# Graph attention heads on one core: one exponential instruction per unit instead of two halves

## The chip, the cores and the metric

The kernel runs on one core of a Trainium2 chip. The metric is the device time in microseconds (us) of one execution; the lower the better.

## The reference, cut to what matters

A graph of 3125 nodes and 103125 edges passes through a graph attention layer with 8 heads, a routed mixture of experts, three more attention layers and a gated feed-forward layer. The change touches only the first attention layer:

```
e = e_left[src] + e_right[dst]
e = jnp.where(e >= 0, e, NEG_SLOPE * e)
e_max = segment_max(e, dst, num_segments=N)
e_exp = jnp.exp(e - e_max[dst])
denom = segment_sum(e_exp, dst, num_segments=N)
alpha = e_exp / (denom[dst] + EPS)
out = segment_sum(Wh[src] * alpha[:, :, None], dst, num_segments=N)
```

## The kernel before, in words

The kernel treats the graph as a dense matrix: a row for each destination node, a column for each source node (3136 columns, NS), and a mask that holds the logarithm of the number of edges between the two. The stage `heads_phase` computes the softmax over the columns and multiplies it with the projected nodes `hx`.

The work is cut into 50 blocks: two passes of 4 heads each (HG), and in each pass 25 blocks of 128 destination nodes. Each head of a block is a unit, so there are 200 units. A unit goes through these steps:

- VectorE, `maxima(u)`: one instruction forms the scores of all 3136 columns into one of three buffers `sc` (L944), and one adds the mask and takes the row's extreme (L948). It first waits until TensorE has transposed the unit that had this buffer three units ago (`s_T`).
- ScalarE, `exps(u, j)`: the exponentials in place, in two halves (L904). Half 0 holds 1664 columns (13 tiles of 128), half 1 holds 1472. Each instruction also leaves the sum of its row in `den`.
- TensorE, `transposes(n)` (L996): the 25 tiles of a unit are turned in four groups of 7, 6, 6 and 6 (TG), n = 4u + gi, into two PSUM buffers `psT` by turns.
- ScalarE, `copy_out(u, gi)` (L913): copies a group from `psT` to `probsT`, two buffers as well.
- TensorE, `products(n)` (L1010): multiplies the copied group into `psO`.

Every engine works through its own queue in a fixed order. TensorE takes `transposes(n + 1)` and then `products(n)`. `transposes(n)` waits until the copy of group n - 2 is out of its buffer; `products(n)` waits for the copy of group n. ScalarE takes, in unit u, copy 0, copy 1, half 0 of the exponentials of unit u + 1, copy 2, copy 3, half 1 of unit u + 1:

```
for gi in range(4):
    copy_out(u, gi)
    if gi % 2 == 1 and u + 1 < UNITS:
        exps(u + 1, gi // 2)
```

VectorE runs two units ahead. Once in a block, after the maxima, `sums(B)` adds the two halves of the denominators (L955), takes their reciprocal (L957) and copies the block's sums out of PSUM into `sumsT` (L959). TensorE turns these with 8 small multiplications (`transpose_sums`, L1017), which stand in its queue behind the last products of the first unit of the next block. `rows(B)` (L967) multiplies with the reciprocals, and GpSimd stores the block.

Of the kernel before, what the change touches and what calls it, by code (L numbers as in the profile page):

```python
# [8 lines left out]
ALU = mybir.AluOpType  # L9
ACT = mybir.ActivationFunctionType  # L10
AX = mybir.AxisListType

P = 128
# [8 lines left out]
NS = SA * SC  # L22
# [14 lines left out]
HG = P // CH  # L37
# [780 lines left out]
CUT = T0[2] * P  # L818
# [4 lines left out]
def heads_phase(nc, g, hx, el, mask, y_dram):  # L823

    with ExitStack() as ctx:
        sb = lambda n, s, d=F32: ctx.enter_context(nc.sbuf_tensor(f"hd_{n}", s, d))
        sem = lambda n: new_semaphore(nc, g, f"hd_{n}")
        sc = sb("scores", [P, 3, NS])
        lv = sb("loops", [LOOP_R[1], 4, LOOP_Q])
        pT = sb("probsT", [P, 2, 7 * P])  # L830
        nm = sb("negmax", [P, 3])
        den = sb("den", [P, 3, HG, 2])
        rden = sb("rden", [P, 3, HG])
        spare = sb("spare", [1, 1])
        oT = sb("sumsT", [P, HG, P])
# [2 lines left out]
        psT = [ctx.enter_context(nc.psum_tensor(f"hd_psT{i}", [P, 1024], F32)) for i in range(2)]  # L838
        psO = [ctx.enter_context(nc.psum_tensor(f"hd_psO{i}", [P, 512], F32)) for i in range(3)]
        psY = ctx.enter_context(nc.psum_tensor("hd_psY", [P, 512], F32))  # L840
        names = ("s_leaky", "s_nm", "s_exp", "s_turned", "s_copied", "s_products", "s_sum", "s_rden", "s_y", "s_oT", "s_yT",
                 "s_fold", "s_loop_in", "s_loop_exp", "s_loop_plus_one", "s_loop_ln", "s_loop_new", "s_loop_out", "s_loop_kept")
        s_lk, s_nm, s_ex, s_T, s_ev, s_mm, s_sum, s_rd, s_y, s_oT, s_yT, s_fold, s_lin, s_lexp, s_lone, s_lln, s_lneg, s_lout, s_lkept = (
            sem(n) for n in names)
        s_mask = [sem(f"s_mask{i}") for i in range(2)]
        s_store = [sem(f"s_store{i}") for i in range(3)]
# [3 lines left out]
        UNITS = BLOCKS * HG  # L850
        CG = P // CH
        LOOP_UNIT = 6
        assert LOOP_UNIT + 1 < HG * (L1_LOOPS // P - 2)
        halves = (slice(0, CUT), slice(CUT, NS))

        def load_el(eng, q, h, i):

# [37 lines left out]

        @block.scalar
        def _(act):
            def exps(u, j):
                B, k = u // HG, u % HG
                if j == 0:  # L900
                    act.wait_ge(s_nm, u + 1)
                    if k == 0 and B >= 3:
                        act.wait_ge(s_y, B - 2)
                nc.scalar.activation(sc[:, u % 3, halves[j]], sc[:, u % 3, halves[j]], ACT.Exp, scale=-1.0,  # L904
                                     bias=nm[:, u % 3:u % 3 + 1], accum_out=den[:, B % 3, k, j:j + 1]).then_inc(s_ex, 1)

            def copy_out(u, gi):
                n = u * 4 + gi
                act.wait_ge(s_T, n + 1)
                if n >= 2:  # L910
                    act.wait_ge(s_mm, n - 1)
                w = TG[gi] * P
                nc.scalar.activation(pT[:, gi % 2, 0:w], psT[gi % 2][:, 0:w], ACT.Copy).then_inc(s_ev, 1)  # L913

            exps(0, 0)
            exps(0, 1)
            for u in range(UNITS):
                if u == LOOP_UNIT:
                    act.wait_ge(s_lin, 16)
                    nc.scalar.activation(lv[:, 1, :], lv[:, 0, :], ACT.Exp, scale=-1.0).then_inc(s_lexp, 1)  # L920
                if u == LOOP_UNIT + 1:
                    act.wait_ge(s_lone, 1)
                    nc.scalar.activation(lv[:, 2, :], lv[:, 2, :], ACT.Ln).then_inc(s_lln, 1)
                for gi in range(4):
                    copy_out(u, gi)
                    if gi % 2 == 1 and u + 1 < UNITS:
                        exps(u + 1, gi // 2)

        @block.vector
        def _(dve):  # L930
            nc.vector.tensor_reduce(fold[:, :], g["ident"][:, :].rearrange("p (j c) -> p c j", c=CH), AX.X,
                                    ALU.add).then_inc(s_fold, 1)

            def maxima(u):
                B, h, c = u // HG, u % HG, u % 3
                q, b = B // NB, B % NB
                if h == 0 and B >= 2:
                    dve.wait_ge(s_mask[B % 2], 16 * (B // 2))
                if b == 0 and q:
                    dve.wait_ge(s_el[h], 32 * q)  # L940
                if u >= 3:
                    dve.wait_ge(s_T, 4 * (u - 2))
                o = D + q * HG + h
                nc.vector.scalar_tensor_tensor(sc[:, c, :], el[:, h, 0, :], hx[:, b, o:o + 1], el[:, h, 1, :],  # L944
                                               ALU.subtract, ALU.min).then_inc(s_lk, 1)
                dve.wait_ge(s_lk, u + 1)
                nc.vector.memset(spare[:, :], 0.0)
                nc.vector.tensor_tensor_reduce(out=sc[:, c, :], in0=sc[:, c, :], in1=mask[:, B % 2, :],  # L948
                                               scale=1.0, scalar=3.0e38, op0=ALU.add, op1=ALU.min,
                                               accum_out=nm[:, c:c + 1]).then_inc(s_nm, 1)  # L950

            def sums(B):
                i = B % 3
                dve.wait_ge(s_ex, (B + 1) * HG * 2)
                nc.vector.tensor_tensor(rden[:, i, :], den[:, i, :, 0], den[:, i, :, 1], ALU.add).then_inc(s_sum, 1)  # L955
                dve.wait_ge(s_sum, B + 1)
                nc.vector.reciprocal(rden[:, i, :], rden[:, i, :]).then_inc(s_rd, 1)  # L957
                dve.wait_ge(s_mm, (B + 1) * HG * 4)
                nc.vector.tensor_copy(oT[:, :, :].rearrange("p h n -> p (h n)"), psO[i][:, 0:HG * P]).then_inc(s_oT, 1)  # L959

            def rows(B):
                i = B % 3
                dve.wait_ge(s_yT, B + 1)
                dve.wait_ge(s_rd, B + 1)
                if B >= 3:
                    dve.wait_ge(s_store[i], 16 * (B // 3))
                nc.vector.tensor_tensor(y[:, i, :].rearrange("p (h c) -> p h c", h=HG),  # L967
                                        psY[:, 0:P].rearrange("p (h c) -> p h c", h=HG),
                                        rden[:, i, :].rearrange("p (h o) -> p h o", o=1).broadcast_to([P, HG, CH]),
                                        ALU.mult).then_inc(s_y, 1)  # L970
            maxima(0)
            maxima(1)
            for u in range(UNITS):
                if u + 2 < UNITS:
                    maxima(u + 2)
                if u % HG == 0 and u:
                    sums(u // HG - 1)
                elif u % HG == 1 and u > HG:
                    rows(u // HG - 1)
            sums(BLOCKS - 1)  # L980
            rows(BLOCKS - 1)

        @block.tensor
        def _(pe):
            pe.wait_ge(s_fold, 1)

            def transposes(n):
                u, gi = n // 4, n % 4
                if gi % 2 == 0:
                    pe.wait_ge(s_ex, u * 2 + gi // 2 + 1)  # L990
                if n >= 2:
                    pe.wait_ge(s_ev, n - 1)
                for t in range(TG[gi]):
                    c0 = (T0[gi] + t) * P
                    r = min(P, NS - c0)
                    last = nc.tensor.transpose(psT[gi % 2][0:r, t * P:(t + 1) * P], sc[:, u % 3, c0:c0 + r], g["ident"][:, :])  # L996
                last.then_inc(s_T, 1)

            def products(n):
                u, gi = n // 4, n % 4  # L1000
                B, h = u // HG, u % HG
                pe.wait_ge(s_ev, n + 1)
                if gi == 0 and h == 0 and B >= 3:
                    pe.wait_ge(s_y, B - 2)
                c0 = (B // NB * HG + h) * CH
                for t in range(TG[gi]):
                    tt = T0[gi] + t
                    r = min(P, NS - tt * P)
                    cg = tt % CG
                    last = nc.tensor.matmul(psO[B % 3][cg * CH:(cg + 1) * CH, h * P:(h + 1) * P], hx[0:r, tt, c0:c0 + CH],  # L1010
                                            pT[0:r, gi % 2, t * P:(t + 1) * P], start=tt < CG, stop=tt >= sum(TG) - CG)
                last.then_inc(s_mm, 1)

            def transpose_sums(B):
                pe.wait_ge(s_oT, B + 1)
                for h in range(HG):
                    last = nc.tensor.matmul(psY[:, h * CH:(h + 1) * CH], oT[:, h, :], fold[:, :], start=True, stop=True)  # L1017
                last.then_inc(s_yT, 1)
            transposes(0)
            for n in range(UNITS * 4):  # L1020
                if n + 1 < UNITS * 4:
                    transposes(n + 1)
                products(n)
                if n % (4 * HG) == 3 and n > 4 * HG:
                    transpose_sums(n // (4 * HG) - 1)
            transpose_sums(BLOCKS - 1)
# [1111 lines left out]
```

## Time and profile before

| | |
|---|---|
| median of 3 runs | 3909.28 us (3903.76 to 3923.56) |
| profiled execution, its own time | 3912.36 us |
| its span | 3910.7 us |
| busy: PE, DVE, ACT, POOL | 3470.7, 2890.0, 2387.8, 233.7 us |
| granted TensorE clock, mean over the span | 0.959 |
| heads stage, first score instruction to last | 520.0 to 1945.5 us |

PE is TensorE, PEld its loading of weights, DVE VectorE, ACT ScalarE, POOL GpSimd. The engines run beside each other, so busy times don't add up to the span. A clock of 1.00 is the 2.4 GHz level, 0.50 the 1.2 GHz level; other values are means over a stretch.

### The profile page before, as it was taken

How to read it: one execution, taken by the hardware profiler on the slowest of the kernel's cores; microseconds unless marked ns; L12 is line 12 of the kernel's file. 1: busy time of each engine (PE TensorE's matmuls, PEld its weight loads, DVE VectorE, ACT ScalarE, POOL GpSimd, SP SyncE). 2: the span in 40 equal slices, each digit the busy share in tenths (PEclk: the TensorE clock that was granted, in tenths of full speed). 3: DMA queues.
4: the chain of work that ended last, by engine and by line, in shares of the span. 5: the costliest groups of instructions: out<-in, count | busy, mean ns of one | idle time of the engine just before them, and what ended most of it. 6: DMA issues, size and time to landing. Idle time of an engine off the chain costs nothing. (4 is left out here: it accounts for less than half of the span.)

```text
span 3910.7 us, 69756 instructions
## 1 busy us (share of the span) xinstructions
PE 3470.7 (89%) x27387; PEld 2703.4 (69%) x27388; DVE 2890.0 (74%) x4413; ACT 2387.8 (61%) x3738; POOL 233.7 (6%) x230
## 2 busy tenths in 40 slices
PE   4998978888888889888937999699999999999699
PEld 3555546666666666666636899688878887888577
DVE  5999999999999999999853222465556555555485
ACT  3777778888888888888810011266656665444432
POOL 1000000000000000000002444100000000000010
PEclk8999999999999999999958999899999999999899
DMA  3423211111115111111166787332323322333210
GB/s 98 184 99 126 100 65 54 70 53 56 67 53 202 53 70 53 55 68 53 37 215 204 217 240 199 91 130 106 109 71 128 114 101 78 137 116 116 66 56 33
DMA packets 153038, 404.77 MB, mean 104 GB/s; under 512 B 20453, under 2 KB 98664, under 8 KB 134664
## 3 DMA queue, kind: packets, MB, share of 16 engines
q1 hardware_dynamic: 133682, 360.65, 26.4%
q0 software_dynamic: 15552, 36.16, 3.9%
q8 instruction: 223, 3.65, 0.4%
q10 hardware_dynamic: 3478, 3.46, 0.3%
q14 instruction: 103, 0.84, 0.1%
HBM read 335.03 MB, written 65.19 MB: 102 GB/s over the span
## 5 line engine op out<-in xcount | busy, mean ns | idle before, releaser
L913 ACT ACTIVATE hd_probsT<-hd_psT 128x768 f32<-128x768 f32 (+1 forms) x800 | 649.1, 836 | 183.8 <-PE hd_psT L996 183.0
L996 PE MATMUL hd_psT<-ident,hd_scores 128*128 128x128 f32 (+1 forms) x5000 | 737.9, 286 | 12.8 <-ACT hd_scores L904 12.8
L944 DVE SCALAR_TENSOR_TENSOR hd_scores<-el_heads,hx 128x3136 f32<-128x3136 f32 x200 | 695.6, 3478 | 0.0
L948 DVE CUSTOM_DVE_ANT_0 hd_scores<-hd_scores,mask_heads 128x3136 f32<-128x3136 f32 x200 | 684.1, 3420 | 8.6
L1010 PE MATMUL hd_psO<-hd_probsT,hx 128*32 128x128 f32 (+1 forms) x10000 | 582.9, 286 | 98.3 <-ACT hd_probsT L913 97.6
L996 PEld LDWEIGHTS hd_psT<-ident,hd_scores 128*128 128x128 f32 (+1 forms) x5000 | 544.3, 143 | 166.7 <-issue 164.5
L904 ACT ACTIVATE hd_scores<-hd_scores,hd_negmax 128x1664 f32<-128x1664 f32 (+1 forms) x400 | 640.7, 1602 | 8.2 <-DVE hd_negmax L948 8.1
L1458 PE MATMUL ly_psO<-hx_a,ly_probsT 128*128 128x256 f32 x2500 | 583.7, 381 | 0.0
L1416 ACT ACTIVATE ly_probsT<-ly_psT 128x768 f32<-128x768 f32 (+1 forms) x300 | 249.6, 832 | 469.0 <-PE ly_psT L1447 468.8
L1010 PEld LDWEIGHTS hd_psO<-hd_probsT,hx 128*32 128x32 f32 (+1 forms) x10000 | 322.6, 110 | 296.9 <-ACT hd_probsT L913 173.6
L1458 PEld LDWEIGHTS ly_psO<-hx_a,ly_probsT 128*128 128x128 f32 x2500 | 453.8, 189 | 71.3 <-issue 16.6
L480 DVE TENSOR_SCALAR onehot_c<-iotaC,stage_c 128x392 bf16<-128x392 f16 x1200 | 295.0, 315 | 0.0
L1458 PE MATMUL ly_psO<-hx_b,ly_probsT 128*128 128x256 f32 x1250 | 292.0, 381 | 0.0
L538 PE MATMUL cnt<-onehot_c,onehot_dst_a 128*128 128x392 bf16 x1200 | 236.8, 334 | 52.4 <-DVE onehot_c L480 52.4
L1447 PE MATMUL ly_psT<-ident,ly_scores 128*128 128x128 f32 x1875 | 258.3, 276 | 16.7 <-ACT ly_scores L1407 16.7
L538 PEld LDWEIGHTS cnt<-onehot_c,onehot_dst_a 128*128 128x128 bf16 x1200 | 135.2, 128 | 171.4 <-issue 76.2
L1407 ACT ACTIVATE ly_scores<-ly_scores,ly_negmax 128x1664 f32<-128x1664 f32 (+1 forms) x150 | 239.6, 1597 | 20.5 <-DVE ly_negmax L1303 10.4
L1303 DVE CUSTOM_DVE_ANT_0 ly_scores<-ly_scores,ly_mask 128x3136 f32<-128x3136 f32 x73 | 249.7, 3420 | 3.1
L1458 PEld LDWEIGHTS ly_psO<-hx_b,ly_probsT 128*128 128x128 f32 x1250 | 226.8, 189 | 35.6 <-issue 8.3
L1447 PEld LDWEIGHTS ly_psT<-ident,ly_scores 128*128 128x128 f32 x1875 | 219.0, 141 | 44.1 <-ACT ly_scores L1407 17.2
L1817 PEld LDWEIGHTS moe_ps_h<-moe_xT,moe_w 128*128 128x128 f32 x2048 | 241.3, 194 | 5.5 <-DVE moe_xT L1858 2.3
L1852 ACT ACTIVATE moe_hidden<-moe_ps_h 128x512 f32<-128x512 f32 x64 | 38.2, 597 | 337.0 <-PE moe_ps_h L1817 263.2
(328 smaller groups left out, 3902.6 us busy)
## 6 DMA issues: line engine op xcount, KB each, us to landing
ly_mask<-mask_dram SPq DMA_DIRECT2D x75, 1568.0 KB, 6.6
mask_heads<-mask_dram SPq DMA_DIRECT2D x48, 1568.0 KB, 7.0
moe_w<-in_L_ffn_w SPq DMA_DIRECT2D x144, 512.0 KB
mask_dram<-logc SPq DMA_DIRECT2D x200, 196.0 KB, 1.9
el_heads<-el_dram POOLq DMA_DIRECT2D x4, 1568.0 KB, 19.1
el_heads<-el_slope_dram POOLq DMA_DIRECT2D x4, 1568.0 KB, 22.7
el_heads<-el_dram SPq DMA_DIRECT2D x4, 1568.0 KB, 11.5
el_heads<-el_slope_dram SPq DMA_DIRECT2D x4, 1568.0 KB, 14.9
```

The source lines that it names most:

```text
L480: last = nc.vector.tensor_scalar(oc[:, k, :], g["iotaC"][:, :], c[:, k:k + 1], None, ALU.is_equal)
L538: last = nc.tensor.matmul(o, ohA[:, s, :, k], ohC[:, s, k, :], start=k == 0 and not further, stop=True, skip_group_check=True)
L904: nc.scalar.activation(sc[:, u % 3, halves[j]], sc[:, u % 3, halves[j]], ACT.Exp, scale=-1.0, bias=nm[:, u % 3:u % 3 + 1], accum_out=den[: ...
L913: nc.scalar.activation(pT[:, gi % 2, 0:w], psT[gi % 2][:, 0:w], ACT.Copy).then_inc(s_ev, 1)
L944: nc.vector.scalar_tensor_tensor(sc[:, c, :], el[:, h, 0, :], hx[:, b, o:o + 1], el[:, h, 1, :], ALU.subtract, ALU.min).then_inc(s_lk, 1)
L948: nc.vector.tensor_tensor_reduce(out=sc[:, c, :], in0=sc[:, c, :], in1=mask[:, B % 2, :], scale=1.0, scalar=3.0e38, op0=ALU.add, op1=ALU.m ...
L996: last = nc.tensor.transpose(psT[gi % 2][0:r, t * P:(t + 1) * P], sc[:, u % 3, c0:c0 + r], g["ident"][:, :])
L1010: last = nc.tensor.matmul(psO[B % 3][cg * CH:(cg + 1) * CH, h * P:(h + 1) * P], hx[0:r, tt, c0:c0 + CH], pT[0:r, gi % 2, t * P:(t + 1) * P ...
L1303: nc.vector.tensor_tensor_reduce(out=sc[:, c, :], in0=sc[:, c, :], in1=mask[:, B % 2, :], scale=1.0, scalar=3.0e38, op0=ALU.add, op1=ALU.m ...
L1416: nc.scalar.activation(pT[:, gi % 2, 0:w], psT[gi % 2][:, 0:w], ACT.Copy).then_inc(s_ev, 1)
L1447: last = nc.tensor.transpose(psT[gi % 2][0:r, t * P:(t + 1) * P], sc[:, B % 3, c0:c0 + r], g["ident"][:, :])
L1458: last = nc.tensor.matmul(psO[B % 2][:, 0:D], pT[0:r, gi % 2, t * P:(t + 1) * P], hx[B // NB % 2][0:r, tt, 0:D], start=tt == 0, stop=tt == ...
```

## The change

The exponentials of a unit become one instruction over all 3136 columns, issued where half 0 stood, behind the second copy. The denominators have one value for each head, so the addition in `sums` and its semaphore go. TensorE waits once per unit for the exponentials, ahead of its first group of transposes.

```diff
-        den = sb("den", [P, 3, HG, 2])
+        den = sb("den", [P, 3, HG])
...
-            def exps(u, j):
+            def exps(u):
                 B, k = u // HG, u % HG
-                if j == 0:
-                    act.wait_ge(s_nm, u + 1)
-                    if k == 0 and B >= 3:
-                        act.wait_ge(s_y, B - 2)
-                nc.scalar.activation(sc[:, u % 3, halves[j]], sc[:, u % 3, halves[j]], ACT.Exp, scale=-1.0,
-                                     bias=nm[:, u % 3:u % 3 + 1], accum_out=den[:, B % 3, k, j:j + 1]).then_inc(s_ex, 1)
+                act.wait_ge(s_nm, u + 1)
+                if k == 0 and B >= 3:
+                    act.wait_ge(s_y, B - 2)
+                nc.scalar.activation(sc[:, u % 3, :], sc[:, u % 3, :], ACT.Exp, scale=-1.0,
+                                     bias=nm[:, u % 3:u % 3 + 1], accum_out=den[:, B % 3, k:k + 1]).then_inc(s_ex, 1)
...
-            exps(0, 0)
-            exps(0, 1)
+            exps(0)
...
-                    if gi % 2 == 1 and u + 1 < UNITS:
-                        exps(u + 1, gi // 2)
+                    if gi == 1 and u + 1 < UNITS:
+                        exps(u + 1)
...
-                dve.wait_ge(s_ex, (B + 1) * HG * 2)
-                nc.vector.tensor_tensor(rden[:, i, :], den[:, i, :, 0], den[:, i, :, 1], ALU.add).then_inc(s_sum, 1)
-                dve.wait_ge(s_sum, B + 1)
-                nc.vector.reciprocal(rden[:, i, :], rden[:, i, :]).then_inc(s_rd, 1)
+                dve.wait_ge(s_ex, (B + 1) * HG)
+                nc.vector.reciprocal(rden[:, i, :], den[:, i, :]).then_inc(s_rd, 1)
...
-                if gi % 2 == 0:
-                    pe.wait_ge(s_ex, u * 2 + gi // 2 + 1)
+                if gi == 0:
+                    pe.wait_ge(s_ex, u + 1)
```

## Rows read from the trace of the kernel before

**Rows 1.** The page's costliest groups: count, busy us, mean ns, idle before.

```profile
L944 DVE SCALAR_TENSOR_TENSOR hd_scores<-el_heads,hx 128x3136 f32<-128x3136 f32 x200 | 695.6, 3478 | 0.0
L948 DVE CUSTOM_DVE_ANT_0 hd_scores<-hd_scores,mask_heads 128x3136 f32<-128x3136 f32 x200 | 684.1, 3420 | 8.6
```

**Rows 2.** Heads stage as one window: length, busy PE, PEld, DVE, ACT, POOL, clock, DMA.

```profile
520.00:1945.70 1425.70, 1260.16 (x15247) 898.63 (x15247) 1415.43 (x997) 1235.41 (x1593) 32.26 (x53) 0.97 0.19 67
```

**Rows 3.** Waits of TensorE from 560 to 1940 us: total, times, longest.

```profile
PE hd_psO L1010 <- ACT hd_probsT L913: 92.3, 177, 1.7
PE hd_psY L1017 <- DVE hd_sumsT L959: 59.2, 47, 2.8
```

**Rows 4.** Timeline of one unit: start us, us, engine, line, operation [idle before].

```profile
1006.08 1.68 ACT L904 ACTIVATE hd_scores<-hd_scores,hd_negmax 128x1664 f32<-128x1664 f32 x1
...
1007.74 1.50 ACT L913 ACTIVATE hd_probsT<-hd_psT 128x768 f32<-128x768 f32 x2
...
1008.59 0.63 PE L1010 MATMUL hd_psO<-hd_probsT,hx 128*32 128x128 f32 x12 [0.52 <-ACT hd_probsT L913]
...
1009.15 0.98 PE L996 MATMUL hd_psT<-ident,hd_scores 128*128 128x128 f32 x7
...
1010.07 0.96 PE L1010 MATMUL hd_psO<-hd_probsT,hx 128*32 128x128 f32 x12
...
1010.96 0.87 PE L996 MATMUL hd_psT<-ident,hd_scores 128*128 128x128 f32 x6
...
1011.87 0.81 ACT L913 ACTIVATE hd_probsT<-hd_psT 128x768 f32<-128x768 f32 x1 [0.31 <-PE hd_psT L996]
...
1012.58 1.67 ACT L904 ACTIVATE hd_scores<-hd_scores,hd_negmax 128x1664 f32<-128x1664 f32 x1
```

**Rows 5.** Timeline around a block's end, VectorE and TensorE.

```profile
1937.68 0.16 DVE L955 TENSOR_TENSOR hd_rden<-hd_den 128x4 f32<-128x4 f32 x1
1937.87 0.18 DVE L957 RECIPROCAL hd_rden<-hd_rden 128x4 f32<-128x4 f32 x1
...
1938.54 3.48 DVE L944 SCALAR_TENSOR_TENSOR hd_scores<-el_heads,hx 128x3136 f32<-128x3136 f32 x1
...
1938.68 1.08 PE L1017 MATMUL hd_psY<-hd_fold,hd_sumsT 128*128 128x32 f32 x8 [0.66 <-DVE hd_sumsT L959]
...
1939.60 0.85 PE L996 MATMUL hd_psT<-ident,hd_scores 128*128 128x128 f32 x6
```

**Rows 6.** ScalarE's groups by shape, whole span: busy us, mean ns, idle before.

```profile
L904 ACT ACTIVATE hd_scores<-hd_scores,hd_negmax 128x1664 f32<-128x1664 f32 x200 | 335.2, 1676 | 8.2 <-DVE hd_negmax L948 8.1
L904 ACT ACTIVATE hd_scores<-hd_scores,hd_negmax 128x1472 f32<-128x1472 f32 x200 | 305.5, 1527 | 0.0
...
L1420 ACT ACTIVATE ly_y<-ly_y 128x256 f32<-128x256 f32 x50 | 20.9, 417 | 11.6 <-DVE ly_y L1352 11.1
...
L774 ACT ACTIVATE hx_b<-hx_b 128x1280 f32<-128x1280 f32 x5 | 5.9, 1257 | 0.0
```

**Rows 7.** Timeline: first exponentials, second copy of the last unit, last row.

```profile
526.98 1.68 ACT L904 ACTIVATE hd_scores<-hd_scores,hd_negmax 128x1664 f32<-128x1664 f32 x1 [6.02 <-DVE hd_negmax L948]
...
1953.49 0.81 ACT L913 ACTIVATE hd_probsT<-hd_psT 128x768 f32<-128x768 f32 x1 [0.32 <-PE hd_psT L996]
...
1959.95 0.29 DVE L967 TENSOR_TENSOR hd_y_stage<-hd_psY,hd_rden 128x128 f32<-128x128 f32 x1 [1.17 <-PE hd_psY L1017]
```

**Rows 8.** Timeline of TensorE at three places, for its pauses and durations.

```profile
590.54 0.63 PE L1010 MATMUL hd_psO<-hd_probsT,hx 128*32 128x128 f32 x12 [1.67 <-ACT hd_probsT L913]
...
1453.61 1.08 PE L1017 MATMUL hd_psY<-hd_fold,hd_sumsT 128*128 128x32 f32 x8 [1.58 <-DVE hd_sumsT L959]
...
1456.82 1.49 PE L996 MATMUL hd_psT<-ident,hd_scores 128*128 128x128 f32 x6
```

**Rows 9.** Windows around two of these pauses, columns as in rows 2.

```profile
588.00:596.00 8.00, 6.33 (x80) 4.57 (x79) 7.96 (x5) 7.67 (x9) 0.63 (x2) 1.00 0.16 11
1456.00:1458.00 2.00, 2.00 (x20) 1.54 (x15) 1.96 (x3) 2.00 (x2) 0.00 (x0) 0.50 0.03 8
```

More of the change, by code:

```diff
@@ L840, in heads_phase @@
         psY = ctx.enter_context(nc.psum_tensor("hd_psY", [P, 512], F32))
-        names = ("s_leaky", "s_nm", "s_exp", "s_turned", "s_copied", "s_products", "s_sum", "s_rden", "s_y", "s_oT", "s_yT",
+        names = ("s_leaky", "s_nm", "s_exp", "s_turned", "s_copied", "s_products", "s_rden", "s_y", "s_oT", "s_yT",
                  "s_fold", "s_loop_in", "s_loop_exp", "s_loop_plus_one", "s_loop_ln", "s_loop_new", "s_loop_out", "s_loop_kept")
-        s_lk, s_nm, s_ex, s_T, s_ev, s_mm, s_sum, s_rd, s_y, s_oT, s_yT, s_fold, s_lin, s_lexp, s_lone, s_lln, s_lneg, s_lout, s_lkept = (
+        s_lk, s_nm, s_ex, s_T, s_ev, s_mm, s_rd, s_y, s_oT, s_yT, s_fold, s_lin, s_lexp, s_lone, s_lln, s_lneg, s_lout, s_lkept = (
             sem(n) for n in names)
@@ L853, in heads_phase @@
         assert LOOP_UNIT + 1 < HG * (L1_LOOPS // P - 2)
-        halves = (slice(0, CUT), slice(CUT, NS))
         def load_el(eng, q, h, i):
```

## The prediction

> **What bounds the kernel now.** I began with the page's costliest groups. The change touches only the heads stage, and there two VectorE instructions stand at the top with next to no idle time before them [rows 1]. The window over the stage settles it: of 1425.7 us VectorE was busy 1415.4, TensorE 1260.2 and ScalarE 1235.4 [rows 2]. So VectorE bounds the stage, at 1425.7 / 50 = 28.51 us for a block of four units, or 7.13 us for a unit.
>
> The waits of TensorE show how the others follow it. Between 560 and 1940 us TensorE waited 59.2 us, once in a block, for the sums that VectorE copies out, and 92.3 us for copies by ScalarE [rows 3]. The first is slack against VectorE: 59.2 / 47 = 1.26 us in a block. So ScalarE and TensorE would need about 27.25 us for a block if VectorE were free. They are only 4% short of being the bound themselves, and what matters is not how busy they are but how long their loop is.
>
> The timeline of one unit shows that loop [rows 4]. ScalarE's half 0 starts at 1006.08; copy 2 starts behind it at 1007.74, 1.66 later. Products 2 start at 1008.59, 0.85 later; TensorE had paused 0.52 us for that copy. Then transposes 0 of the next unit at 1009.15 (0.56 later), products 3 at 1010.07 (0.92), transposes 1 at 1010.96 (0.89), copy 1 at 1011.87 (0.91, waiting for those transposes), and half 0 again at 1012.58 (0.71). The terms close: 1.66 + 0.85 + 0.56 + 0.92 + 0.89 + 0.91 + 0.71 = 6.50 us. Each step is released by the one before it, or stands behind it in the queue. Half 0 is in this loop and half 1 is not: half 1 runs while TensorE does transposes 0 and products 3.
>
> **The change part by part.**
>
> *The merged instruction.* It is put where half 0 stood, in the loop, with all the columns. The trace has no exponential of 3136 columns. The two halves give a slope of (1676 - 1527) / 192 = 0.776 ns for a column, hence 1676 + 1472 x 0.776 = 2818 ns; the two shapes of the other activation function give (1257 - 417) / 1024 = 0.820, hence 1676 + 1472 x 0.820 = 2883 ns [rows 6]. Above, it can't well cost more than the two halves together, 3203 ns; below, not less than the 2818, since the smaller slope already takes the short form's 1527 as it is. I take 2.87, near the second slope, which rests on wider shapes. The next instruction started 0.02 us before the end of half 0 [rows 4], so the advance is 2.85 us.
>
> The Trainium skill ("ScalarE: Activation LUTs", What ACT_TABLE_LOAD costs) prices an activation with a per-partition bias at about 280 ns plus 0.833 ns an element. By the page that would be an estimate of 2.89 us, and the loop would be 0.02 us longer than with my value. The page's price for one instruction more speaks for the merge as far as ScalarE's busy time goes.
>
> ScalarE does save: two instructions advanced 1.66 and 1.51 (1.53 less the same 0.02) and one advances 2.85, 0.32 us in a unit. But ScalarE's busy time bounds nothing, before or after; the saving falls into idle time and I count it as nothing. If ScalarE's own queue were the bound it would be 200 x 0.32 = 64 us.
>
> *The loop with it.* Copy 2 now stands behind 2.85 instead of 1.66 us: the loop becomes 6.50 + 1.19 = 7.69 us. I looked for what could take up the 1.19. TensorE pauses already when it waits for copy 2, so nothing on it covers the delay: its pause grows from 0.52 to 1.71. Transposes 3 are done by then. Copy 3 follows copy 2 and is ready before products 3. Copy 0 of the next unit used to stand behind half 1 and now waits only for transposes 0; at little over the 0.81 us of a six-tile copy [rows 4] it ends before products 0 come up, 1.8 us after it can start, and copy 1 is released by transposes 1 as before. So the whole 1.19 stays.
>
> *The block.* 7.69 is more than VectorE's 7.13 for a unit, so the bound passes from VectorE to the loop. Once in a block the eight small multiplications stand in the loop: from their start to the transposes behind them 1939.60 - 1938.68 = 0.92 us, and they no longer wait, since VectorE has a unit's time to copy the sums [rows 5]; I take 0.9. A block costs 4 x 7.69 + 0.9 = 31.7 us against 28.51.
>
> *The addition removed.* Reciprocals started 0.19 us after the additions [rows 5]; 50 x 0.19 = 9.5 us of VectorE. While VectorE was the bound this was worth 9.5 us. Behind the new bound it is covered by VectorE's new idle time, some 3 us in a block, and I count nothing.
>
> *Waits and queues.* TensorE's single wait ahead of transposes 0 is satisfied 1.4 us before they come up (copy 2 and products 2 lie between), nothing. VectorE's wait for a free score buffer now ends last: it starts maxima of unit u + 3 when the transposes of unit u are done, needs 6.9 to 7.9 us, and ScalarE wants the result two loops later; it can't be late. Mask loads and stores follow VectorE and only get more time. No DMA is added.
>
> *Start and end.* From the first exponential (526.98) to copy 1 of the last unit it is 200 loops and 49 blocks' small multiplications, less what the first and last unit don't have: no copy 2 and products 2 between the first exponentials and their transposes (0.85 + 0.56 = 1.4), and no exponential behind that copy 1 (0.7). So copy 1 comes at 526.98 + 1538.0 + 44.1 - 1.4 - 0.7 = 2107.0. From there to the last row's end nothing changes: 1959.95 + 0.29 - 1953.49 = 6.75 [rows 7]. The stage ends at 2113.7 instead of 1960.2: **153.5 us later**. The stages behind it are untouched. The profiled execution took 3912.4, which makes 4066; it lay 3.1 above the median of the runs shown, so for the median I say 3909.3 + 153.5 = **4063 us**, 3.9% slower. With the exponential at 2.82 or 2.90 us it would be 10 us less or 6 more, and 0.1 us of error in the small multiplications is 5 us: 4045 to 4080 as this case's own range.
>
> **The rivals.**
>
> *Hidden after all (the other side).* If the loop stayed below VectorE's pace, the stage would gain what the addition cost: 3909 - 9.5 = 3900 us, within 0.5% of before. It needs 4 x (4.84 + x) + 0.9 < 28.3 for an advance x of the merged instruction, so x < 2.01 us. At 2.01, 3136 columns would run at less than the time that the slope alone asks (2.43 us). Only a loop that I have misread, with copy 2 not needed so soon, could bring this. Chance 4%.
>
> *No saving by the merge.* If the merged instruction takes the sum of its halves, 3.20, with an advance of 3.18, the loop is 8.02 us: 200 x 0.33 = 66 us more, 4129. The slopes speak against it. 5%.
>
> *The clock falls.* The trace has places where TensorE's granted clock goes to 0.50: behind a pause of 1.58 us with the eight small multiplications after it, and six transposes then took 1.49 instead of 0.87 us [rows 4, 8, 9]. The new pauses of 1.71 us come 200 times. Against it: behind a pause of 1.67 us ahead of products 2 the clock stayed at 1.00 [rows 8, 9], with the very kinds of work that will surround the new pauses. But 1.71 is a little longer. TensorE's part of the loop is 0.56 + 0.92 + 0.89 + 0.91 = 3.3 us; at 1.49 / 0.87 = 1.7 times that it is 2.3 us more for a pause with a fall behind it. With one pause in three that is 67 x 2.3 = 154 us more: 4217. The Trainium skill ("TensorE: Matmul & The Clock Gate", A second HAM failure mode: psum-queue depth-cycling) says that short idle stretches between groups of matmuls can make the clock go up and down; by that rule this case would come in, and the 1.67 us row doesn't yet show it. 12%.
>
> **How the numbers follow.** My forecast 79%, clock 12%, no saving 5%, hidden 4%. The likeliest gives 4063. For eight in ten I take in the exponential's upper bound and a few falls of the clock: 4040 to 4130, which leaves out hidden and most of the clock's case. About 0.5% (20 us) is what a measurement of this kernel can tell from no change. Slower by more than that: all but hidden and a part kept for a loop misread by half, 94%; same 5%; faster 1%.
>
> **What would show it.** Right: exponentials near 2.87 us, unit to unit 7.69 us; TensorE waits for copies about 200 x 1.7 = 340 us instead of 92, and no longer for the sums; VectorE's score instruction gets idle time, some 150 us, released by transposes; a block of 31.7 us. Wrong: VectorE without idle time (hidden), exponentials of 3.2 (no saving), a mean clock in the stage well under 0.97 (clock).

## The result, and the profile after

The changed kernel takes 4173.5 us, median of 4 runs (4134.4 to 4178.5), against 3908.0 us before: ratio 1.0653, 95% interval 1.061 to 1.0696. That is 265 us slower. I had forecast slower, at 4063 us with a range to 4130; the time lies above the range.

First the page's costliest groups of the kernel after, the ones that answer to [rows 1] and [rows 6]. The columns are count, busy us, mean ns, idle time before and what ended it:

```profile
L911 ACT ACTIVATE hd_probsT<-hd_psT 128x768 f32<-128x768 f32 (+1 forms) x800 | 646.5, 835 | 498.1 <-PE hd_psT L991 498.1
...
L941 DVE SCALAR_TENSOR_TENSOR hd_scores<-el_heads,hx 128x3136 f32<-128x3136 f32 x200 | 696.7, 3484 | 259.3 <-PE hd_psT L991 258.7
...
L902 ACT ACTIVATE hd_scores<-hd_scores,hd_negmax 128x3136 f32<-128x3136 f32 x200 | 580.3, 2902 | 6.0 <-DVE hd_negmax L945 6.0
```

Two things are to be seen. The merged exponential takes 2902 ns. And VectorE, which had next to no idle time before, now has 259 us of it before its first score instruction, all of it ended by transposes on TensorE: the bound has moved from VectorE to the loop.

The stage as one window, as in [rows 2]. Columns: length; busy time and count of PE, PEld, DVE, ACT, POOL; granted clock; DMA share; GB/s:

```profile
520.00:2235.00 1715.00, 1354.60 (x15400) 960.53 (x15400) 1425.33 (x950) 1207.71 (x1205) 33.78 (x54) 0.92 0.16 56
```

The last row of the stage, to be laid beside [rows 7]:

```profile
2234.82 0.29 DVE L962 TENSOR_TENSOR hd_y_stage<-hd_psY,hd_rden 128x128 f32<-128x128 f32 x1 [1.17 <-PE hd_psY L1012]
```

It ended at 2235.1 us instead of 1960.2, 274.9 later. (What follows the stage was 8.7 us shorter in this execution than in the one before, 1941.7 for 1950.4 us. No kernel of this document changes that part, and over their twelve profiled executions it took 1941.7 to 1950.5 us, so this is the spread from one execution to the next.) VectorE's busy time is nearly what it was, 1425.3 us for 1415.4. The clock is lower, 0.92 for 0.97.

The waits of TensorE from 540 to 2215 us, as in [rows 3]. The wait for VectorE's sums is gone, and the one for ScalarE's copies has grown more than threefold:

```profile
PE hd_psO L1005 <- ACT hd_probsT L911: 343.9, 196, 3.2
```

Now the timeline of two units in a row, to be laid beside [rows 4]:

```profile
1101.91 2.90 ACT L902 ACTIVATE hd_scores<-hd_scores,hd_negmax 128x3136 f32<-128x3136 f32 x1
...
1104.81 1.50 ACT L911 ACTIVATE hd_probsT<-hd_psT 128x768 f32<-128x768 f32 x2
...
1105.65 0.63 PE L1005 MATMUL hd_psO<-hd_probsT,hx 128*32 128x128 f32 x12 [1.75 <-ACT hd_probsT L911]
...
1106.22 1.50 PE L991 MATMUL hd_psT<-ident,hd_scores 128*128 128x128 f32 x7
...
1107.65 1.62 PE L1005 MATMUL hd_psO<-hd_probsT,hx 128*32 128x128 f32 x12
...
1109.21 1.21 PE L991 MATMUL hd_psT<-ident,hd_scores 128*128 128x128 f32 x6
...
1111.16 2.90 ACT L902 ACTIVATE hd_scores<-hd_scores,hd_negmax 128x3136 f32<-128x3136 f32 x1
...
1114.91 0.63 PE L1005 MATMUL hd_psO<-hd_probsT,hx 128*32 128x128 f32 x12 [1.75 <-ACT hd_probsT L911]
...
1115.47 0.98 PE L991 MATMUL hd_psT<-ident,hd_scores 128*128 128x128 f32 x7
...
1117.27 1.08 PE L1012 MATMUL hd_psY<-hd_fold,hd_sumsT 128*128 128x32 f32 x8
...
1119.78 2.90 ACT L902 ACTIVATE hd_scores<-hd_scores,hd_negmax 128x3136 f32<-128x3136 f32 x1
```

The order is the one that I had worked out: the exponential, copy 2 behind it, products 2 released by that copy after a pause of 1.75 us, and so on round. But the first unit takes 9.25 us and the second 8.62, which has the eight small multiplications in it and is 7.7 without them. In the first, seven transposes take 1.50 us instead of 0.98, and the products 1.62 instead of 0.96. Windows over the same stretch say why:

```profile
1104.00:1106.00 2.00, 0.34 (x10) 0.35 (x12) 2.00 (x1) 2.00 (x4) 0.00 (x0) 1.00 0.00 0
1106.00:1108.00 2.00, 2.00 (x23) 1.45 (x18) 1.96 (x3) 0.55 (x2) 0.00 (x0) 0.63 0.04 8
1108.00:1110.00 2.00, 2.00 (x16) 1.20 (x9) 2.00 (x1) 0.68 (x1) 0.00 (x0) 0.52 0.00 0
1112.00:1120.00 8.00, 6.25 (x81) 4.66 (x72) 6.76 (x3) 5.40 (x7) 0.00 (x0) 1.00 0.00 0
```

TensorE stood still for most of the first window; in the two behind it the granted clock is at 0.50 for most of the time, the 1.2 GHz level. Behind the same pause in the next unit it stays at 1.00. In the trace's record of the clock there are 72 such falls in the stage, 249 us at 0.50; in the kernel before there are 18, 61 us. (The stage is counted here without its start, where in every kernel the clock is at 0.50 until about 535 us.) Experiment 6 will show that the 18 cost nothing.

So two questions were open: is the loop what I took it for, and is the clock what lies above my sum?

### The profile page after: what moved, and what is told of

Read it like the earlier page. It is cut to its first block and busy times, and to the rows that moved or that the text cites. A ratio compares the mean times of both kernels' runs of the same rounds, so it can differ in the third digit from the quotient of the medians.

```text
span 4176.8 us, 69106 instructions
## 1 busy us (share of the span) xinstructions
PE 3552.3 (85%) x27387; PEld 2757.3 (66%) x27388; DVE 2897.9 (69%) x4363; ACT 2351.2 (56%) x3338; POOL 234.4 (6%) x230
## 5 line engine op out<-in xcount | busy, mean ns | idle before, releaser
L1005 PE MATMUL hd_psO<-hd_probsT,hx 128*32 128x128 f32 (+1 forms) x10000 | 626.4, 299 | 349.4 <-ACT hd_probsT L911 349.4
L991 PE MATMUL hd_psT<-ident,hd_scores 128*128 128x128 f32 (+1 forms) x5000 | 779.6, 297 | 14.0 <-ACT hd_scores L902 14.0
L1005 PEld LDWEIGHTS hd_psO<-hd_probsT,hx 128*32 128x32 f32 (+1 forms) x10000 | 341.8, 113 | 571.4 <-ACT hd_probsT L911 403.4
L991 PEld LDWEIGHTS hd_psT<-ident,hd_scores 128*128 128x128 f32 (+1 forms) x5000 | 578.3, 149 | 176.6 <-issue 172.4
L902 ACT ACTIVATE hd_scores<-hd_scores,hd_negmax 128x3136 f32<-128x3136 f32 x200 | 580.3, 2902 | 6.0 <-DVE hd_negmax L945 6.0
L1812 PE MATMUL moe_ps_h<-moe_xT,moe_w 128*128 128x128 f32 x2048 | 241.1, 276 | 1.7 <-DVE moe_xT L1853 1.0
```

Of the source, the lines that this page charges most:

```text
L902: nc.scalar.activation(sc[:, u % 3, :], sc[:, u % 3, :], ACT.Exp, scale=-1.0, bias=nm[:, u % 3:u % 3 + 1], accum_out=den[:, B % 3, k:k + 1 ...
L1812: last = nc.tensor.matmul(out[:, m * P:(m + 1) * P], w12[:, t % WS, i, k, m * P:(m + 1) * P], xT[:, t % 2, k, :], start=k == 0, stop=k == 1)
```

## The experiments

All times are medians. Each ratio is to runs of the kernel before on the same chip, whose medians were 3906.8 to 3911.0 us.

**1. The pause filled.** Ten transposes of the identity are added to the changed kernel behind the fourth group of every unit, into columns of `psT` that nobody reads. They also hold back the signal that this group is done.

```diff
                 for t in range(TG[gi]):
...
+                if gi == 3:
+                    for _ in range(10):
+                        last = nc.tensor.transpose(psT[1][:, 7 * P:8 * P], g["ident"][:, :], g["ident"][:, :])
                 last.then_inc(s_T, 1)
```

> The changed kernel with ten more 128x128 transposes of the identity behind the fourth group of each unit, written to columns of psT that nobody reads (their result is left out of everything). They lie in TensorE's pause of 1.75 us ahead of products 2 and last about 1.35 us. Theory (the loop is longer, and behind the pauses the clock falls 71 times at about 1.5 us each): no falls in the stage, granted clock there near 1.00, loop still 7.74 us, time 4066 us (4055 to 4080). Rival (what is above my sum comes from something else in the longer loop, and the clock is an accompaniment): the time stays at 4170 or rises with the added work.

Measured: 4074.2 us (4068.0 to 4078.4), ratio 1.0423, interval 1.0402 to 1.0444. More work on TensorE, and 99 us less time. The timeline of this kernel:

```profile
1102.38 2.90 ACT L902 ACTIVATE hd_scores<-hd_scores,hd_negmax 128x3136 f32<-128x3136 f32 x1
...
1104.22 1.26 PE L994 MATMUL hd_psT<-ident 128*128 128x128 f32 x10
...
1106.13 0.63 PE L1008 MATMUL hd_psO<-hd_probsT,hx 128*32 128x128 f32 x12 [0.66 <-ACT hd_probsT L911]
```

and its stage as a window:

```profile
520.00:2126.00 1606.00, 1460.78 (x17396) 1114.19 (x17396) 1425.67 (x950) 1207.62 (x1205) 32.48 (x54) 0.99 0.17 60
```

Products 2 still wait for copy 2, but the pause is 0.66 us instead of 1.75, and the clock is 0.99. Only one fall is left in the stage, behind a pause of 2.08 us near its start. From the first to the last exponential it took 1583.3 us against 1694.5 in the changed kernel: 111 us for 71 falls, 1.57 us a fall. The changed kernel says the same by itself: of its units without the small multiplications, the 79 without a fall take 7.73 us and the 67 with one 9.30 us (medians), 1.57 more. The loop without a fall is unchanged in the filled kernel, 7.72 us, so the signal held back costs nothing. The rival, that the clock only accompanies something else, is out.

**2. The pause shortened a little.** The same with two added transposes (`range(2)`).

> As the run with ten added transposes, but with two: the pause shrinks from 1.75 to about 1.48 us. If the clock depends on how long the pause is, and 1.67 us stood without a fall in the kernel before, most falls go: 4066 to 4100 us. If any pause of over a microsecond can bring the fall, most of the 107 us stay: 4140 or more.

Measured: 4076.5 us (4069.6 to 4084.3), ratio 1.0432, interval 1.0407 to 1.0456. One fall in the stage, as with ten. The pause in its timeline:

```profile
1104.76 0.63 PE L1008 MATMUL hd_psO<-hd_probsT,hx 128*32 128x128 f32 x12 [1.53 <-ACT hd_probsT L911]
```

A pause of 1.53 us, with 0.38 us of work put ahead of it, leaves the clock alone; of 195 pauses of 1.75 us 71 had a fall behind them (the changed kernel's other fall stands behind a pause of 3.17 us near the start). So in this loop little separates the two cases. Experiment 7 will show that the length of the pause alone is not what decides.

**3. The merged exponential behind copy 0.**

```diff
-                    if gi == 1 and u + 1 < UNITS:
+                    if gi == 0 and u + 1 < UNITS:
                         exps(u + 1)
```

> The changed kernel with the merged exponentials issued behind copy 0 instead of copy 1. Theory (position in the loop decides): the loop runs exponentials, copy 1, products 1, transposes 3, copy 3, then the next unit; worked through with the steps of the trace it is 7.57 us, and the eight small multiplications lie beside the exponentials and cost nothing more; TensorE's longest pause is about 0.8 us, so no falls of the clock. Stage 83 us longer than before: 3992 us (3975 to 4010). Rival (the merge as such costs, wherever it stands): 4130 to 4175.

Measured: 3986.0 us (3984.4 to 3986.8), ratio 1.0198, interval 1.0181 to 1.0215. The instruction is the same, and only its place in ScalarE's queue is another: 188 us less than behind copy 1. Beside experiment 1, where the clock stands too, it is 88 us less, and that is what the place costs by itself; the rest is the falls. Its timeline over one unit:

```profile
1102.25 2.90 ACT L902 ACTIVATE hd_scores<-hd_scores,hd_negmax 128x3136 f32<-128x3136 f32 x1
...
1105.99 0.63 PE L1005 MATMUL hd_psO<-hd_probsT,hx 128*32 128x128 f32 x12 [1.53 <-ACT hd_probsT L911]
...
1109.75 2.91 ACT L902 ACTIVATE hd_scores<-hd_scores,hd_negmax 128x3136 f32<-128x3136 f32 x1
```

The loop is 7.50 us, and nearly every unit has it (195 of 199 intervals), those with the small multiplications too: these now lie beside the exponential. The time was expected within 6 us, but the pause wasn't: I had said about 0.8 us, and it is 1.53. The clock stood all the same (0.99 in the stage; two falls, behind pauses of over 3 us near its start), at a pause as long as in experiment 2 and without added work.

**4. The move without the merge.** Both halves behind copy 1, in the kernel before; the addition stays.

```diff
-                    if gi % 2 == 1 and u + 1 < UNITS:
-                        exps(u + 1, gi // 2)
+                    if gi == 1 and u + 1 < UNITS:
+                        exps(u + 1, 0)
+                        exps(u + 1, 1)
```

> The kernel before with both halves issued behind copy 1, the addition kept: the move without the merge. Theory: the loop has 1.66 + 1.51 = 3.17 us of exponentials in it, hence 8.01 us; 200 x 0.27 = 54 us more than the changed kernel, plus as many or more falls of the clock behind pauses of 2.0 us: 4230 us (4210 to 4290). Rival (merging made one slow instruction, and moving is harmless): near 3908.

Measured: 4313.0 us (4310.6 to 4329.4), ratio 1.105, interval 1.1022 to 1.1079. The rival is out: the move alone costs more than the change did. But the time lies 23 us beyond my own upper bound. TensorE's pause and the stage:

```profile
1104.05 0.63 PE L1011 MATMUL hd_psO<-hd_probsT,hx 128*32 128x128 f32 x12 [2.02 <-ACT hd_probsT L913]
```

```profile
520.00:2363.00 1843.00, 1466.17 (x15392) 1031.54 (x15392) 1433.68 (x999) 1262.12 (x1604) 32.97 (x53) 0.86 0.15 52
```

The clock is 0.86: 113 falls, 505 us at 0.50. Of 157 pauses of 2.02 us 112 had a fall behind them, a larger share than of those of 1.75, and the clock stays low longer at a time (505 / 113 = 4.5 us for 249 / 72 = 3.5). Whether the falls explain the whole excess is the next experiment.

**5. The same, with the pause filled.** Four added transposes, as in experiments 1 and 2 (`range(4)`), on the kernel of experiment 4.

> Both halves behind copy 1, not merged (as in the run that took 4313 us), with four added transposes of the identity that nobody reads in TensorE's pause, which shrinks from 2.02 to about 1.5 us. Theory (loop 8.01 us without a fall of the clock, and what that run lay above its 4128 us were 113 falls): 4074 + 200 x 0.27 = 4128 us (4115 to 4145), clock near 1.00. Rival (the two instructions in a row cost more in the loop than their durations): above 4200.

Measured: 4123.5 us (4122.0 to 4126.6), ratio 1.0549, interval 1.0509 to 1.0589. The pause:

```profile
1108.15 0.63 PE L1014 MATMUL hd_psO<-hd_probsT,hx 128*32 128x128 f32 x12 [1.59 <-ACT hd_probsT L913]
```

Behind the 196 pauses of 1.58 or 1.59 us there is no fall; the two in the stage stand behind pauses of 2.40 and 3.02 us near its start. So the loop, measured at 8.00 us, gives 4124 us, and 190 us of the 4313 were the clock. It also gives the merge by itself: 4123.5 - 4076.5 = 47 us for 200 units, 0.24 us each. The loops of the two traces give 8.00 - 7.72 = 0.28, and the durations say 1.66 + 1.51 - 2.90 = 0.27.

**6. How much the loop can take.** The kernel before, with the cut between the halves moved, so that 19 or 15 of the 25 tiles are exponentiated behind copy 1 instead of 13.

```diff
-        halves = (slice(0, CUT), slice(CUT, NS))
+        halves = (slice(0, 19 * P), slice(19 * P, NS))
```

> The kernel before with the cut of the exponentials moved from column 1664 to 2432, so that 19 of 25 tiles are exponentiated behind copy 1 and 6 behind copy 3. Theory (only the length of the instruction behind copy 1 is in the loop): 1676 + 768 x 0.833 = 2316 ns, advance 2.30, loop 7.14 us, block 4 x 7.14 + 0.9 = 29.5 against 28.51, TensorE's pause 1.16 us and no falls: 48 us more, 3956 us. Rival (up to the merge nothing is lost, since ScalarE's busy time stays the same): 3908.

> The kernel before with the cut at column 1920 (15 tiles behind copy 1, 10 behind copy 3). Theory: advance 1.66 + 256 x 0.833 = 1.87 us, loop 6.71, block 4 x 6.71 + 0.9 = 27.7 us, still under VectorE's 28.51: no change, 3907 us, while TensorE waits less for the copied sums. Rival (every lengthening of the instruction behind copy 1 is paid): 200 x 0.21 = 42 us more, 3949 us.

Measured with 19 tiles: 3957.0 us (3950.9 to 3970.4), ratio 1.0129, interval 1.0105 to 1.0153. Measured with 15 tiles: 3910.3 us (3902.1 to 3914.5), ratio 1.0, interval 0.9985 to 1.0016. One and the same edit, in two sizes: with 15 tiles the loop is 6.71 us, 0.21 more than before, and that costs nothing; with 19 it is 7.14 us, 0.64 more, and that costs 50 us in all. In between the loop passes VectorE. With 15 tiles only 2 falls of the clock are left of the 18, and the time is the same: in the kernel before the falls lay in TensorE's slack. The waits of TensorE in the kernel with 15 tiles show the slack going, against 59.2 us in [rows 3]:

```profile
PE hd_psO L1010 <- ACT hd_probsT L913: 146.2, 196, 1.9
PE hd_psY L1017 <- DVE hd_sumsT L959: 33.7, 44, 2.6
```

and with 19 tiles it is gone, and VectorE has begun to wait:

```profile
PE hd_psO L1010 <- ACT hd_probsT L913: 227.5, 196, 2.3
PE hd_psY L1017 <- DVE hd_sumsT L959: 1.1, 1, 1.1
```

```profile
DVE hd_scores L944 <- PE hd_psT L996: 26.0, 95, 0.9
```

**7. The addition by itself.** The kernel before, with the addition of the halves on GpSimd.

```diff
+            def add(B):
+                pool.wait_ge(s_ex, (B + 1) * HG * 2)
...
+                nc.gpsimd.tensor_tensor(rden[:, B % 3, :], den[:, B % 3, :, 0], den[:, B % 3, :, 1], ALU.add).then_inc(s_sum, 1)
...
-                nc.vector.tensor_tensor(rden[:, i, :], den[:, i, :, 0], den[:, i, :, 1], ALU.add).then_inc(s_sum, 1)
```

> The kernel before with only the addition of the denominators' halves moved from VectorE to GpSimd. Theory (in the kernel before VectorE bounds the stage, so what leaves its queue comes off the end): 50 x 0.19 = 9.5 us less, 3899 us. Rival (the 0.19 us is hidden, or a wait for GpSimd takes its place): no change.

Measured: 3896.7 us (3896.1 to 3912.4) against 3906.8, ratio 0.9975, interval 0.9962 to 0.9989. The 9.5 us are real as long as VectorE bounds the stage. In the change they could not be had, since it moved the bound away from VectorE.

This trace also bears on the clock. With VectorE's queue shorter, TensorE's pause ahead of the small multiplications is 1.38 us instead of 1.57:

```profile
681.80 1.08 PE L1024 MATMUL hd_psY<-hd_fold,hd_sumsT 128*128 128x32 f32 x8 [1.38 <-DVE hd_sumsT L966]
```

```profile
682.00:686.00 4.00, 4.00 (x33) 3.25 (x33) 3.96 (x3) 1.98 (x2) 0.00 (x0) 0.62 0.02 4
```

In the 4 us from there the granted clock is 0.62. Behind 31 such pauses of 1.37 or 1.38 us there are 14 falls, and in the kernel before 16 behind 28 pauses of 1.57 or 1.58. Ahead of products 2, experiments 2, 3 and 5 had 540 pauses of 1.53 to 1.59 us and not one fall. So the length of the pause alone doesn't decide; what TensorE does around it counts too, and which part of that, no run here separates.

**8. What the profile of before asks for.** VectorE is the bound, and the loop has 1.26 us of slack a block. So the copy of the sums goes from VectorE to ScalarE, behind copy 0 of the next block's first unit, where ScalarE waits for transposes 1 anyway:

```diff
+            def copy_sums(B):
+                act.wait_ge(s_mm, (B + 1) * HG * 4)
+                if B:
+                    act.wait_ge(s_yT, B)
+                nc.scalar.activation(oT[:, :, :].rearrange("p h n -> p (h n)"), psO[B % 3][:, 0:HG * P],
+                                     ACT.Copy).then_inc(s_oT, 1)
...
                     copy_out(u, gi)
+                    if gi == 0 and u % HG == 0 and u:
+                        copy_sums(u // HG - 1)
...
-                nc.vector.tensor_copy(oT[:, :, :].rearrange("p h n -> p (h n)"), psO[i][:, 0:HG * P]).then_inc(s_oT, 1)
...
                 pe.wait_ge(s_oT, B + 1)
+                if B:
+                    pe.wait_ge(s_y, B)
```

> The kernel before with the copy of a block's sums out of PSUM on ScalarE, behind copy 0 of the next block's first unit, instead of on VectorE. Theory: VectorE's block falls from 28.51 to 27.85 us; the loop of ScalarE and TensorE needs 4 x 6.50 + 0.9 and a little for the copy, some 27.2 to 27.5, and no longer waits for VectorE; 50 x 0.66 = 33 us less, 3876 us. Rival (the copy in ScalarE's queue lengthens the loop, as the merge did): gain under 15 us or a loss.

> Both of these: the addition on GpSimd and the copy of the sums on ScalarE. Theory: VectorE's block 27.66 us, still just above the loop's 27.2 to 27.5: 42 us less than before, 3867 us. If the loop is the bound by then: the same as with the copy alone.

Measured: with the copy alone 3873.2 us (3869.1 to 3882.2), ratio 0.9912, interval 0.9896 to 0.9927; with the addition on GpSimd as well 3866.7 us (3859.1 to 3872.2), ratio 0.989, interval 0.9873 to 0.9907. Both beat the kernel before and the changed one. By the medians the addition's gain on top of the copy is 6.5 us, with overlapping ranges. In the two profiled executions the time from the first exponential to the last row is 9.7 us shorter, 1391.9 for 1401.6 us, which is the 9.5 that the sum asks for. The stage of the second:

```profile
520.00:1917.00 1397.00, 1242.23 (x15400) 889.66 (x15400) 1376.74 (x899) 1269.29 (x1654) 137.09 (x104) 1.00 0.19 68
```

VectorE is still the bound (ScalarE waits for it 94 times, 26 us in all, for the row extremes), and no fall of the clock is left.

## Why the prediction was wrong in size

**What bounds the kernel before: right.** Work taken off VectorE came off the time, 10 us of 9.5 and 34 us of 33 (experiments 7 and 8); work put into the loop cost nothing while the loop was the shorter one (experiment 6, 15 tiles).

**The loop with the merged instruction: right, a little short.** The exponential that I had at 2.87 us, with an advance of 2.85, measured 2902 ns and an advance of 2.90. The loop is 7.72 us for 7.69; over 200 units that is 7 us. With the pause shortened (experiment 2) the stage takes 1597.1 us from the first exponential to the last row, where my sum has 1586.7: 10 us more, the 7 and some 3 for the first units, which are irregular and have the one fall that is left. So without the falls the sum was right within these 10 us, and the kernel takes 4074 to 4077 us against my 4063. The slope between 1664 and 3136 columns is (2902 - 1676) / 1472 = 0.833 ns, steeper than both that I had formed. The Trainium skill ("ScalarE: Activation LUTs", What ACT_TABLE_LOAD costs) gives just this for an element, and the estimate of 2.89 us worked out from it was nearer than my 2.87.

**The block, the addition, the waits: right.** The small multiplications cost 8.62 - 7.72 = 0.90 us for my 0.9, without a wait. VectorE idles before its score instruction, released by transposes, for 259 us where I had said some 150; with the pause filled it is 146 us, so the excess is the falls. The addition's 9.5 us are less than this idle time. TensorE's waits for copies came to 343.9 us for my 340.

**The clock: the step that failed.** The sum had the falls of the clock at nothing. I had them as a rival at 12%, and it came in. The step in question is "behind a pause of 1.67 us ahead of products 2 the clock stayed at 1.00 [...] with the very kinds of work that will surround the new pauses. But 1.71 is a little longer". One pause of 1.67 us without a fall was taken to speak for 200 of 1.71, which became 1.75 with the longer exponential. It says little: in the changed kernel, too, 124 of the 195 pauses of 1.75 us had no fall behind them. And the trace of before had 28 pauses of 1.57 or 1.58 us of which 12 had none, so it already showed that only a part of such pauses brings a fall. The runs put in its place: in this loop, ahead of products 2, none behind pauses of 0.66, 1.53 and 1.59 us, 71 behind those of 1.75, 112 behind those of 2.02. The falls cost 1.57 us each, 111 for 71 of them, and 153.5 + 10 + 111 = 274.5 against the measured 274.9 of the stage. The price that the rival gave, 2.3 us a fall, was too high: it let the low clock last through all of TensorE's part of the loop, 3.3 x 1.7 = 5.6 us, and a fall lasts 3.5 us. The share that it gave, one unit in three, was close to the 72 of 200. With the price too high its time, 4217, is 44 us above the measured one.

What the Trainium skill reports of another kernel, whose clock goes up and down over short idle stretches between its groups of matmuls ("TensorE: Matmul & The Clock Gate", A second HAM failure mode: psum-queue depth-cycling), is what happened here: up and down 72 times, all but one behind pauses of 1.75 us. I had set it aside on the strength of one row.

**The rivals on the other side: out.** Hidden needed an advance under 2.01 us; experiment 6 finds the crossing between a measured advance of 1.88 (no change) and 2.31 us (50 us lost), and this kernel has 2.90. That merging saves nothing is out too: it saves 0.24 to 0.28 us a unit.

**The spread of the changed kernel.** Its four runs lie from 4134 to 4179 us, while those of experiments 1 and 2 stay within 15 us. The mean granted clock of each whole execution goes with its time: 0.938, 0.939, 0.942 and 0.950 at 4178.5, 4176.0, 4171.0 and 4134.4 us. A mean of 0.938 is twice 0.062 of the time at 0.50, so between the first and the last there is an estimated 2 x (0.062 x 4177 - 0.050 x 4133) = 105 us less at 0.50. The 71 falls cost 111 us for 246 us at 0.50; by that price the 105 are worth 47 us, and the times differ by 44. So the spread fits a number of falls that changes from run to run.

**Open.** Why 71 of 195 equal pauses bring the clock down and 124 don't. In the profiled execution they are uneven: 4 falls in the 49 units with the small multiplications, 67 in 146 others.

## What to carry to other kernels

When two queues hand work back and forth through two buffers, find the closed chain of releases and ask of every instruction whether it is inside; an instruction inside costs its full length, one beside it nothing, whatever the busy shares say. Merging two instructions saves the fixed part (here 0.27 us), but puts both lengths at one place; here the half that had run beside TensorE's work was moved into the loop. And when a repeated pause of TensorE grows to about the length of one behind which the trace shows a fall of the clock, price the falls in, and don't take one pause without a fall as proof: here two in three had none, and the others cost 111 us. Or put a little work into the pause: two useless transposes a unit took 97 us off the changed kernel.

## What the runs showed of the hardware that I had not expected

How little lies between: in this loop, ahead of products 2, pauses of 1.53 us left the granted clock of the stage at 0.99, pauses of 1.75 us brought it to 0.92, and 2.02 us to 0.86. And the length is not all: ahead of the eight small multiplications, 14 of 31 pauses of 1.38 us had a fall behind them. Added work made a kernel faster (4173.5 to 4074.2 us with 2000 more transposes). And a GpSimd addition of 128x4 elements took 1026 ns in experiment 7 and 2112 ns in experiment 8 (means of 50, and rough, as times on GpSimd are), against 158 ns on VectorE. It did no harm: both kernels gained about what the sum asked for.
